# A fused cross-attention and feed-forward block: forty products of a constant ahead of the first loads, a finer split of the first value weights, and the weight mean moved behind the second chunk's values

## The reference, cut to what matters

```python
x = x + tanh(g_xattn) * attention(layernorm(x), ctx, ctx, W_q, W_k, W_v, W_o, qpos, kpos, mask)
x = x + tanh(g_ffn) * ffn(layernorm(x), W_r, W_k, W_v, mu_r, mu_k)

def attention(query, keys, values, ...):      # 16 batches, 512 queries, 120 keys, 16 heads of 32
    Q, K, V = query @ W_q.T, keys @ W_k.T, values @ W_v.T
    scores = Q K^T / sqrt(32) - slope[h] * (qpos - kpos), masked
    e = exp(scores - max); attn = e / (1 + sum(e))
    return (attn V) @ W_o.T

def ffn(x, ...):                              # x_prev is x one token earlier
    r = sigmoid((mu_r * x + (1 - mu_r) * x_prev) @ W_r)
    k = (mu_k * x + (1 - mu_k) * x_prev) @ W_k
    return r * (relu(k) ** 2 @ W_v)
```

## Time and profile before

| | |
|---|---|
| median of 3 runs | 1311.96 us (1311.15 to 1312.66) |
| profiled execution | 1310.22 us, of which the span from the first to the last instruction is 1308.4 us |
| PE busy | 1282.4 us, 98% of the span |
| DVE busy | 1068.7 us, 82% |
| ACT busy | 837.4 us, 64% |
| POOL busy | 786.9 us, 60% |
| mean granted clock | 0.998 |
| PE in the chain that ended last | 82% |

### The profile page before, as it was taken

How to read it: one execution, slowest core, us unless ns; L and a number is a source line. 1 busy time by engine, 2 the same in 40 slices (tenths; PEclk the granted TensorE clock), 3 DMA queues, 4 the chain that set the end, 5 groups by cost and what they waited for, 6 DMA issues and landing times.

```text
span 1308.4 us, 30826 instructions
## 1 busy us (share of the span) xinstructions
PE 1282.4 (98%) x9848; PEld 1044.2 (80%) x9848; DVE 1068.7 (82%) x2834; ACT 837.4 (64%) x2868; POOL 786.9 (60%) x731
## 2 busy tenths in 40 slices
PE   8999999999999999999999999999999999999998
PEld 7888778878777777877777787778778877878877
DVE  4667988888888888888888888888888888888864
ACT  5357483956758394765839486674839577584942
POOL 0015567676666667666666766666676766667641
PEclk9999999999999999999999999999999999999999
DMA  8762304031221304022120502222040412212000
GB/s 286 218 202 80 104 27 136 0 109 52 73 88 36 125 8 140 12 75 86 52 108 8 153 0 85 75 73 88 32 129 0 118 43 73 88 48 74 9 26 33
DMA packets 75377, 103.74 MB, mean 79 GB/s; under 512 B 26960, under 2 KB 33104, under 8 KB 75344
## 3 DMA queue, kind: packets, MB, share of 16 engines
q1 hardware_dynamic: 75344, 103.31, 25.2%
HBM read 78.62 MB, written 24.67 MB: 79 GB/s over the span
## 4 chain that ended last, share of the span: by engine, by line
PE 82%; DVE 6%; DMA 5%; issue 4%; POOL 2%; DVEq 0%; ACT 0%; POOLq 0%; SPq 0%
PE rotating L504 58%; PE score_bank L583 5%; PE probs_bank L677 4%; PE attn_bank L688 4%; PE attn_bank L677 4%; DMA rstd_row<-rstd_scratch 4%; PE score_bank L504 4%; PE score_bank L599 1%; DMA rstd_scratch<-rstd 1%; DVE norm L1221 1%; DVE mix_k L1231 1%; POOL rstd L1452 1%; DVE gated L1248 1%; DVE attn_t L1192 1%; PE probs_bank L599 1%
## 5 line engine op out<-in xcount | busy, mean ns | idle before, releaser
L877 ACT ACTIVATE probs<-probs,neg_max 128x120 f32<-128x120 f32 x1024 | 390.7, 388 | 3.6 <-DVE neg_max L1177 3.5
L1471 POOL TENSOR_TENSOR probs<-probs,recip 128x960 f32<-128x960 f32 x128 | 232.1, 1813 | 162.6 <-DVE recip L1188 162.6
L1173 DVE SCALAR_TENSOR_TENSOR probs<-mask_in,score_bank 128x120 f32<-128x120 f32 x1024 | 213.6, 270 | 27.6 <-PE score_bank L583 26.3
L504 PE MATMUL rotating<-w_proj,attn_t 128*128 128x512 f32 x768 | 192.9, 400 | 7.0 <-DVE attn_t L1192 7.0
L877 ACT ACTIVATION_READ_ACCUMULATOR probs<-probs,neg_max 128x1 f32 x1024 | 197.1, 192 | 0.0
L504 PE MATMUL rotating<-w_gate,mixed_gate 128*128 128x512 f32 x768 | 195.2, 400 | 1.2 <-DVE query_t L1158 1.1
L504 PE MATMUL rotating<-w_value,xt_or_act 128*128 128x512 f32 x720 | 180.8, 400 | 0.0
L504 PE MATMUL rotating<-mixed_key,w_key 128*128 128x512 f32 x720 | 178.7, 397 | 0.0
L504 PE MATMUL rotating<-xt_or_act,w_query 128*128 128x512 f32 x744 | 177.3, 394 | 0.0
L504 PEld LDWEIGHTS rotating<-w_proj,attn_t 128*128 128x128 f32 x768 | 140.8, 188 | 42.8 <-issue 12.5
L1177 DVE TENSOR_REDUCE neg_max<-probs 128x4 f32<-128x480 f32 x256 | 167.2, 653 | 8.8
(11 more groups left out here) (126 smaller groups left out, 2205.9 us busy)
## 6 DMA issues: line engine op xcount, KB each, us to landing
x_again<-in_x_dram SPq DMA_DIRECT2D x64, 256.0 KB, 2.7
xt_raw<-in_x_t_dram SPq DMA_DIRECT2D x16, 1024.0 KB, 8.0
xs<-in_x_dram SPq DMA_DIRECT2D x64, 256.0 KB, 5.4
out_dram<-gated SPq DMA_DIRECT2D x64, 256.0 KB, 2.0
rstd_row<-rstd_scratch SPq DMA_DIRECT2D x16, 256.0 KB, 5.3
value_scratch<-gated SPq DMA_DIRECT2D x16, 240.0 KB, 3.6
mask_in<-in_mask_dram SPq DMA_DIRECT2D x16, 240.0 KB, 2.9
keys_t<-key_scratch SPq DMA_DIRECT2D x16, 240.0 KB, 4.8
```

Source lines behind the costliest of these rows:

```text
L504: mm = pe.matmul(bank, stationary(a, c), moving(b, c), start=(i == 0), stop=(i == MATMULS - 1))
L877: e = act.activation(probs[:, t % 2, head, :], probs[:, t % 2, head, :], ACT.Exp, bias=neg_max[:, t % 2, head:head + 1], accum_out=sums[:, ...
L1173: z = dve.scalar_tensor_tensor(out=probs[:, t % 2, head, :], in0=neg_dist[:, t, :], scalar=SLOPES[head], in1=score_banks[j][:, g * NK:(g + ...
L1471: pool.tensor_tensor(part, part, recip[:, t % 2, heads].unsqueeze(2).to_broadcast((P, H // 2, NK)), ALU.mult)\
```

## The change

There are three edits.

- POOL fills `column_mean` as its first instruction, and PE multiplies this tile with itself 40 times into a corner of `attn_bank` before it waits for the first pieces. Nothing reads the result.
- The value weights of the first chunk come in four pieces, not two: four DMA issues, four high parts on ACT, four low parts on DVE, and V0 goes in four steps of six products with a wait each. The semaphore counts of the last piece go from 8 to 10.
- PE makes V1 before the mean. On DVE `values_out(0)` goes ahead of `weight(2)`, and `values_out(1)` ahead of the wait for the mean.

```diff
+WARM_UP = 40
...
-                        (xs[:, 1, 0:2], wv_split[:, :, 0:2]), (xs[:, 1, 2:4], wv_split[:, :, 2:4])]
+                        *((xs[:, 1, c:c + 1], wv_split[:, :, c:c + 1]) for c in range(CT))]
...
                 elif i == 3:
-                    sp.wait_ge(piece_low, 8)
+                    sp.wait_ge(piece_low, 10)
...
+            pe.wait_ge(column_mean_ready, 1)
+            for _ in range(WARM_UP):
+                pe.matmul(attn_bank[:, 0:P], column_mean[:], column_mean[:], start=True, stop=True)
...
-            for half in range(2):
-                pe.wait_ge(piece_low, 7 + half)
+            for c in range(CT):
+                pe.wait_ge(piece_low, 7 + c)
                 for b in range(CB):
                     mm = product(rotating[b][0:NK, :], lambda s, c: ctx_split[0][:, s, c, b * NK:(b + 1) * NK],
-                                 lambda s, c: wv_split[:, s, c, :], range(half * MATMULS // 2, (half + 1) * MATMULS // 2))
-                    if half == 1:
+                                 lambda s, c: wv_split[:, s, c, :], range(c * passes, (c + 1) * passes))
+                    if c == CT - 1:
                         mm.then_inc(vproj_done, 1)
             chunk_keys(1)
-            pe.wait_ge(column_mean_ready, 1)
+            chunk_values(1)
             pe.wait_ge(weight_low, 1)
...
             mm.then_inc(column_mean_done, 1)
-            chunk_values(1)
...
             dve.tensor_copy(qpos_f[:], qpos_in[:]).then_inc(qpos_ready, 1)
+            values_out(0)
             weight(2)
-            values_out(0)
             chunk(2)
+            values_out(1)
             dve.wait_ge(column_mean_done, 1)
...
-            values_out(1)
...
+            pool.memset(column_mean[:].bitcast(F32), 1.0 / D).then_inc(column_mean_ready, 1)
             pool.memset(ident[:], 0.0).then_inc(ident_zero, 1)
...
-            pool.memset(column_mean[:].bitcast(F32), 1.0 / D).then_inc(column_mean_ready, 1)
```

More of the change, by code:

```diff
@@ L177, in flamingo_block @@
         small_loaded = sem("small_loaded")
-        piece_loaded = [sem(f"piece_loaded{i}") for i in range(8)]
+        piece_loaded = [sem(f"piece_loaded{i}") for i in range(10)]
         piece_high = sem("piece_high")
@@ L365, in _ @@
             for i, src in enumerate((first_ctx[:, 0:2], first_wk[:, 0:1], first_wk[:, 1:2], first_ctx[:, 2:4],
-                                     first_wk[:, 2:3], first_wk[:, 3:4], first_wv[:, 0:2], first_wv[:, 2:4])):
+                                     first_wk[:, 2:3], first_wk[:, 3:4], *(first_wv[:, c:c + 1] for c in range(CT)))):
                 sp.dma_start(first_pieces[i][0], src).then_inc(piece_loaded[i], 16)
@@ L1039, in batch @@
                 mix_gate_high(b, 3)
-            for i in range(8):
+            for i in range(10):
                 piece(i)
```

## The result

| | before | changed |
|---|---|---|
| median of 7 runs | 1311.55 us | 1316.25 us (1315.22 to 1316.97) |
| ratio | 1 | 1.0033, 95% interval 1.0022 to 1.0045 |
| span of the profiled execution | 1308.4 us | 1313.5 us |

The kernel became 4.7 us slower by the medians, and 0.33% by the ratio; the forecast was 1310.3 us.

A forecast was written before the change was run, and what follows sets the result against it. PE was taken to bound the kernel (82% of the chain); V0 ending at 17.53 instead of 19.26 us gives 1.73 us, carried through from a median of 1311.96 to 1310.3 us, with an 8-in-10 range of 1309.2 to 1312.3 us.

The forecast's parts named there:

- What bounds the kernel: Whole kernel: PE is 82% of the chain, so PE work done earlier at the start carries through; K0 loses 2.64 us.
- The forty products: Before K0 on PE: forty products at 0.12 us each, 4.8 us in all, from about 1.0 us to 5.8 us.
- The clock: Start of PE: the clock rises from 1.2 to 2.4 GHz 5.0 us after PE starts, at 6.0 us.
- The rival with 4%: Start: weight loads in line, clock stays low, forty products take 8.8 us, 4.1 us lost, 1316.1 us; chance 4%.
- The loads' schedule: K0 and V0: K0's steps wait for pieces ready at 7.24 and 9.20 us; K0 ends at 11.94, V0 at 17.53 us.
- Edits worth 0.3 us: V0: with halves PE would wait 0.3 us for the value weights, with four pieces not at all; already in the sum.
- the cover at K3: Before K3: chunk 3 is ready at about 40.3 us and K3 starts at 41.34 us, 1.0 us of cover.
- the mean's move: V1 before the mean on PE: worth nothing by itself, as PE waits for nothing in either order.
- The gain of 1.7 us: V0's end moves from 19.26 to 17.53 us, 1.73 us earlier, and all that follows on PE shifts by it.
- the bounds 0.115 and 0.22 us: Price of one 128-column product at the slow clock: 0.115 us scaled by columns from 240, 0.22 us from the transposes.
- 2.64 us: K0: its time beyond K1's, read as the slow clock's cost; the ceiling of the gain, 1309.3 us, more than forecast 4%.

The follow-up runs named there:

- the bf16 run: The changed kernel with the forty products on a bf16 tile of 128 x 128 in place of the fp32r one; they took 4.4 us, V0 ended at 17.42 us.
- the wide one: The changed kernel with ten products of 512 columns in place of forty of 128, moving operand a second constant tile; ratio 0.9986.

## Why the prediction was wrong

**What bounds the kernel** held. PE's start carries through: the shift of V0's end, 2.89 us, is 2.87 us at batch 0's last transposes (147.99 against 145.12 us). K0's extra time was the clock's: every version that raised it before K0 or in its first products had K0 end at 11.9 to 12.1 us, against 13.1 to 13.7 us with no products or with twenty.

**The forty products: the step that failed** is "I take 0.12 us, near the lower end". It measured 0.220 us, the upper bound. The argument for it, that the 240-column product "already shows that its weight load hides (0.112 us against 100 ns of columns)", misread the row. 0.112 us at the full clock and 0.216 us at the slow one are not 240 columns with something left over; they are the weight load, 0.11 and 0.22 us, with 240 columns just hidden behind it: at the slow clock 64, 128 and 240 multiplied columns cost 0.218, 0.220 and 0.216 us. The transposes in the earlier trace rows had the same price, 0.11 us for 128 columns at the full clock, though with plain fp32 operands, so that this row alone can't tell load from columns. To scale a product's time by its columns was wrong as long as its weights were not scaled too. The Trainium skill's rule in "TensorE: Matmul & The Clock Gate", section "LDWEIGHTS (loading the stationary operand)", gives 107 ns for 128 columns. The fp32r runs do not agree (0.22 us at 1.2 GHz), and the measurement decides; the bf16 run, 0.11 us a product, doesn't contradict it but can't test it, since the product's own columns can take that time.

**The clock: failed too**, and by the same error. "If the clock rises 5.0 us after PE starts, as before" took PE's activity as one kind, and the delay as fixed. After 8.8 us of products at 0.22 us for 128 columns each, the clock was at 1.2 GHz still, in four profiles, and rose only 2.6 to 5.0 us after K0's first product. With the same columns at 0.107 us it rose 3.2 to 3.8 us after the first product in the three profiles with 64 weight columns, and 5.6 us after it in the bf16 one (4.9 us in the wide one). With no products or with twenty ahead, it rose 3.8 to 4.9 us after K0's first. Why the delay varies is open; whether the long products helped K0 a little (2.6 and 3.5 us in the two profiles of the changed kernel, 4.8 and 5.0 us in the other two) can't be told.

**The size of the loss.** The rival with 4% had both of its facts right, 0.22 us a product and a clock that stays low, and named the time, 1316.1 us (measured 1316.25). Its mechanism was wrong, since load and product do not stand in line, and the close hit is partly luck: in this pair of profiles K0 took 6.79 us and not 8.03, V0 ended 2.9 us late and not 4.1, and the rest came in the batches. Over more profiles the start alone explains the ratio. Four profiles with the long products had V0 end at 22.15, 22.46, 23.05 and 23.22 us, mean 22.72; three whose start had no help (before, no products, twenty) at 19.26, 18.80 and 18.64, mean 18.90. The difference is 3.8 us, or 0.29%, beside measured ratios of 1.0033, 1.0029 and 1.0023. The pair of single profiles showed less at the start (2.89 us) and 2.2 us more behind it; most of the latter is the batch wait's count, 12 against 9 at 0.6 us each, which varied as much among kernels with no such edit.

**The loads' schedule held in its sum, not in its parts.** With the clock up, V0 ended at 17.42 to 17.68 us in four profiles with the four pieces; 17.53 was forecast. But the forecast had PE wait almost nothing for the third piece (7.25 to 7.28 us) and 0.6 us for the fifth (8.63 to 9.24 us). In the timed version with 64 weight columns PE waited 0.60 us for the third, whose low part ended at 7.74 us, not at the 7.24 us of the earlier trace rows, and not at all for the fifth. That the two sums agree is partly luck. "Edits worth 0.3 us" was near (about 0.5 us), and so was the cover at K3 (1.0 forecast, 1.1 measured); the mean's move at nothing was seen only together with the four pieces. The gain of 1.7 us was there to be had: the two timed versions with the other edits that raise the clock gained 0.11% and 0.14%, 1.4 and 1.8 us. The third timed one, without them, gained 0.06%, with an interval that reaches no change.

**The forecast's form.** The range ended at 1312.3 us and gave 4% to what happened, although I had the bounds 0.115 and 0.22 us for the one unknown price, and the upper was a row of the same column count. Each of two linked unknowns was given its own small chance; they were one.

## What to carry to other kernels

A TensorE product cost, in these runs, the longer of its weight load and its columns. Before you price a new shape, ask which of the two the nearest row shows: if 240 columns and 128 columns cost the same with weights of one type and width, neither row is about columns. Filler products that are to raise the clock should have few weight columns or 2-byte weights and many columns to multiply (ten of 512 columns, or forty with 64 weight columns, did it; forty of 128 x 128 fp32r did not), and they should end before the first real operand is ready, since every one beyond that is a plain loss. Their value is bounded by the loads behind them: here 1.7 of 2.64 us.

## What the runs showed of the hardware that was not expected

- The load of 128 fp32r weight columns takes 0.22 us at 1.2 GHz. With half the columns a product takes 0.107 us, and with 128 bf16 columns 0.11 us; there the load is that or less. The median load record, which holds more than the load, goes from 333 ns to 223 ns with half the columns and to 151 ns with bf16. By estimate from these records, the load is halved with half the columns, and the bf16 one is well under half of the fp32r one.
- Products of one constant raise the clock like any others: in the wide version K0 ran in 5.91 us against 7.47 without products.
- The granted clock column says 1.00 for the start of every profile, also where products take 415 ns in place of 275. Only durations tell the level there.
- At the end of a batch DVE's `norm` takes 0.53 or 0.54 us in some batches and 1.2 to 1.7 us in others. From the kernel before, a batch of 74.65 us and one of 75.25 us:

```profile
294.59 0.53 DVE L1221 TENSOR_SCALAR norm<-xs,mv,rstd 128x512 f32 x1
```

```profile
368.61 1.07 DVE L1158 SCALAR_TENSOR_TENSOR query_t<-rotating,rstd_row 128x512 f32<-128x512 f32 x1 [0.49 <-DMA rstd_row<-rstd_scratch]
369.38 1.29 POOL L1501 TENSOR_TENSOR mixed_gate<-relu,mixed_gate 128x512 fp32r<-128x512 f32 x1
369.60 1.37 DVE L1221 TENSOR_SCALAR norm<-xs,mv,rstd 128x512 f32 x1
```

In the second, the row of `rstd` lands 0.5 us late, `norm` starts inside a GpSimd operation and ends 0.3 us after it, and PE waits 0.45 us for it; in the first, it starts 0.15 us before that operation. This was only observed; no run was made to test it. At 0.6 us in each of 9 to 14 batches it would be worth 5.4 to 8.4 us by estimate, more than this whole change.
